# One layer's quantised feed-forward moved into the turns of the attention before it, with GpSimd taking over part of the VectorE work

## The reference, cut to what matters

```python
def xattn0(x, ctx):                      # 16 heads of 64, 256 queries, 64 keys
    scores = q @ k.T * 64 ** -0.5        # causal mask, heads side by side: 16 * 64 = 1024 columns
    return softmax(scores) @ v @ WO
def ffn0(h):                             # h = layer-normed x
    amax  = max(abs(h)) over blocks of 32
    scale = 2 ** (floor(log2(amax)) - 2) * 2 ** (0.5 * tanh(4 * delta))
    q     = fp4_round(clip(h / scale, -6, 6)) * scale
    return q @ quantised_weight.T + bias
x = x + tanh(g) * xattn0(layernorm(x), ctx)
x = x + tanh(g) * ffn0(layernorm(x))
```

## Time and profile before

| | us |
|---|---|
| three timed runs | 1154.90, 1156.94, 1159.53 (median 1156.94) |
| the profiled execution: its time, and its span | 1150.98, 1149.2 |
| busy in the span: TensorE, VectorE, ScalarE, GpSimd | 1009.0, 755.2, 491.6, 360.2 |
| granted TensorE clock, mean | 0.932 |
| share of the chain that ended last: TensorE, VectorE, ScalarE, DMA | 67%, 20%, 4%, 4% |

### The profile page before, as it was taken

One profiled execution on the slowest core, in us unless ns is written; L12 is line 12 of the kernel. 1 busy time (PEld: TensorE's weight loads), 2 busy tenths in 40 slices (PEclk: granted clock), 3 DMA queues, 4 the chain that ended last, 5 costly groups with the idle time before them and its releaser, 6 DMA issues.

```text
span 1149.2 us, 17589 instructions
## 1 busy us (share of the span) xinstructions
PE 1009.0 (88%) x6266; PEld 612.9 (53%) x6273; DVE 755.2 (66%) x2259; ACT 491.6 (43%) x951; POOL 360.2 (31%) x406
## 2 busy tenths in 40 slices
PE   9999999985499998899889999999999995399980
PEld 6355665664344445434776666665544443177750
DVE  2657767779976677685777655555678787444334
ACT  2655555554334442364224333332344442266534
POOL 0060000003332283312343422100425765356670
PEclk7999999995699998899989999999999997799995
DMA  8075000004000003000003444433000101501116
GB/s 195 1 271 154 1 1 1 1 6 87 1 2 1 1 1 118 1 0 1 1 1 77 98 93 95 86 75 75 1 1 25 34 32 41 209 30 36 35 45 225
DMA packets 37846, 61.99 MB, mean 54 GB/s; under 512 B 6049, under 2 KB 22152, under 8 KB 36994
## 3 DMA queue, kind: packets, MB, share of 16 engines
q1 hardware_dynamic: 33154, 52.40, 16.8%
q0 software_dynamic: 4608, 8.50, 2.3%
HBM read 40.47 MB, written 21.45 MB: 54 GB/s over the span
## 4 chain that ended last, share of the span: by engine, by line
PE 67%; DVE 20%; ACT 4%; DMA 4%; issue 3%; POOL 1%; SPq 0%; DVEq 0%; POOLq 0%; ACTq 0%
PE bank L1148 8%; PE bank L1210 6%; PE bank L585 5%; PE bank L490 5%; PE bank L447 5%; PE bank L1164 5%; PE bank L1221 3%; PE bank L651 3%; PE bank L418 3%; PE bank L476 2%; PE bank L483 2%; DVE nmax L2099 2%; ACT att L1386 2%; DMA big_a<-gates 1%; PE bank L604 1%
## 5 line engine op out<-in xcount | busy, mean ns | idle before, releaser
L1148 PE MATMUL bank<-big_b 128*128 128x512 f32 x288 | 135.8, 596 | 0.0
L2099 DVE TENSOR_REDUCE nmax<-bank 128x16 f32<-128x1024 f32 x64 | 77.9, 1218 | 46.6 <-PE bank L591 28.6
L1703 POOL TENSOR_SCALAR xn<-xw,mean,rstd 128x128 f32<-128x128 f32 x62 | 49.5, 808 | 181.5 <-DVEq L2674 90.4
L1600 ACT ACTIVATE att<-bank 128x512 f32<-128x512 f32 (+1 forms) x72 | 43.0, 597 | 134.4 <-PE bank L1148 131.9
L1874 POOL DMA_INDIRECT expert_outs<-big_a,big_b x80 | 77.7, 971 | 56.0 <-DVE big_a L2748 32.9
L1164 PEld LDWEIGHTS bank<-big_b,att 128*128 128x128 f32 (+1 forms) x576 | 72.9, 191 | 31.8 <-issue 19.1
L2610 DVE TENSOR_TENSOR att<-att,bank 128x512 f32<-128x512 f32 (+1 forms) x72 | 49.2, 684 | 57.0 <-PE bank L1164 54.2
L1164 PE MATMUL bank<-big_b,att 128*128 128x128 f32 (+1 forms) x576 | 77.9, 278 | 3.5 <-DVE xw L1978 2.2
L1386 ACT ACTIVATE att<-bank 128x1024 f32<-128x1024 f32 x64 | 62.0, 1021 | 41.4 <-PE bank L627 41.4
L1865 POOL DMA_INDIRECT expert_rows<-xw,big_b x64 | 63.7, 995 | 50.6 <-DVEq L2201 34.1
L1210 PE MATMUL bank<-big_b 128*128 128x384 f32 (+1 forms) x192 | 72.8, 522 | 0.7 <-ACT big_b L1627 0.7
(11 more groups left out here) (423 smaller groups left out, 2166.5 us busy)
## 6 DMA issues: line engine op xcount, KB each, us to landing
big_a<-gates SPq DMA_DIRECT2D x14, 1024.0 KB, 9.8
expert_rows<-big_b SPq DMA_DIRECT2D x1, 5240.0 KB, 19.6
expert_outs<-big_b SPq DMA_DIRECT2D x1, 4096.0 KB, 31.9
big_a<-expert_outs SPq DMA_DIRECT2D x6, 512.0 KB, 8.4
big_a<-expert_rows SPq DMA_DIRECT2D x1, 2620.0 KB, 13.8
big_a<-in_mask SPq DMA_DIRECT2D x2, 1024.0 KB, 12.2
big_b<-in_w_in SPq DMA_DIRECT2D x1, 2048.0 KB, 8.1
out<-xw SPq DMA_DIRECT2D x8, 256.0 KB, 2.4
```

The lines of the kernel that those rows point to most:

```text
L1148: mm = nc.tensor.matmul(bank[2 * (n % 3) + k][:, :], w13[:, k, c * 128:(c + 1) * 128], xnT_all[:, g * GW:(g + 1) * GW], start=True, stop=True)
L1703: ins = nc.gpsimd.tensor_scalar(xn[:, b % 2, j], x[:, t], mean[:, t:t + 1], rstd[:, t:t + 1], SUB, MUL)
L2099: nc.vector.tensor_reduce(nmax[:, j], psum[:, 2048:3072].rearrange("p (h t) -> p h t", t=T), AX.X, MAX, negate=True).then_inc(s.free, 1)
```

## The change

Groups 0 to 5 of layer 0's feed-forward run inside turns 3 to 15 of its attention; groups 6 and 7 remain behind it. Group g is normalised in turn 2g+3 (ScalarE, `ffn_norms`) and its scales found there (VectorE, `block_scales`); it is rounded in turn 2g+4 (`rounded`), and transposed and multiplied in two halves in turns 2g+5 and 2g+6 (`half_transposes`, `half_products`), each half followed by its own residual sum on VectorE (`half_output`). GpSimd gets four tasks in the attention: in each turn it normalises the second tile's probabilities; in each even turn it makes mean and inverse root of one group of tiles (`statistics0`, 23 small instructions in a chain) and then multiplies a rounded group by its scale and adds the bias (`rescaled`); in each odd turn it multiplies by the inverse scale (`unscaled`). The mask is loaded in turn 3 and converted in turns 8, 10, 12 and 14. `unrounded` moves from `big_a` to `big_b`. The core of the diff:

```diff
@@ PE, attention0 @@
+                    if b == 1:
+                        weights_transpose()
+                    if b > 4:
+                        half_transposes(*divmod(b - 5, 2))
                     pe.wait_ge(s.v_evac, 2 * b + 2)
                     pe.wait_ge(s.normed, 2 * b + 1)
                     chunk_transposes(0, 0)
                     chunk_transposes(0, 1)
                     if b + 1 < B:
                         score(b + 1, 1, 1).then_inc(s.scores, 1)
+                    if b > 4:
+                        half_products(*divmod(b - 5, 2))
@@ ACT, attention0 @@
                     if b + 2 < B:
                         norms(b + 2)
+                    if b == 1:
+                        weights_evac()
+                    if b > 2 and b % 2:
+                        ffn_norms((b - 3) // 2)
+                    if b > 7 and b % 2 == 0:
+                        masks((b - 8) // 2)
+                    if b > 4:
+                        half_evac(*divmod(b - 5, 2))
                     turned_evac(b, 0)
                     turned_evac(b, 1)
@@ POOL @@
+            def statistics0(g):
+                ...
+                pool.wait_ge(att_sems.nmax, 2 * g + 4)
+                step(tt(apart, me, mo, SUB))
+                ...
+                for _ in range(3):
+                    step(tt(apart, r, r, MUL))
+                    step(tt(apart, apart, v, MUL))
+                    step(ts(apart, apart, -0.5, 1.5, MUL, ADD))
+                    step(tt(r, r, apart, MUL))
+                step(tt(square, mu, r, MUL))
+                ts(square, square, -1.0, None, MUL).then_inc(att_sems.ready, 1)
+            def attention0(s):
+                for b in range(B):
+                    p = probs[:, 1].rearrange("p (h t) -> p h t", t=T)
+                    pool.wait_ge(s.summed, b + 1)
+                    nc.gpsimd.tensor_tensor(p, p, rsum[:, 1, H:2 * H].unsqueeze(2).broadcast_to([128, H, T]), MUL) \
+                        .then_inc(s.normed, 1)
+                    if b > 1 and b % 2 == 0:
+                        statistics0(b // 2 - 1)
+                    ...
+                    if b > 2 and b % 2:
+                        unscaled((b - 3) // 2)
+                    if b > 3 and b % 2 == 0:
+                        rescaled(b // 2 - 2)
@@ POOL, main @@
             blank_rows()
             spread_keys(g1)
+            attention0(att_sems)
             pool.wait_ge(layer_done, 1)
             similarity_keys()
@@ DVE, attention0 @@
                     step(nc.vector.tensor_reduce(rsum[:, j, 0:H], p, AX.X, ADD))
+                    if j:
+                        nc.vector.reciprocal(rsum[:, j, H:2 * H], rsum[:, j, 0:H]).then_inc(s.summed, 1)
+                        return
@@
-                    else:
-                        ...
-                        moments_of(settled)
-                        first_root(settled)
-                        better_root(settled)
+                    if b > 2 and b % 2:
+                        block_scales((b - 3) // 2)
+                    if b > 3 and b % 2 == 0:
+                        rounded(b // 2 - 2)
                     for j in range(2):
-                        ...
                         dve.wait_ge(s.o, 2 * b + j + 1)
                         residual(0, 2 * b + j, bank[7 - 3 * j][:, 0:128], s.o_read, 2 * b + j + 1, statistics=False)
+                        if b > 4 and j == 0:
+                            half_output(*divmod(b - 5, 2))
```

More of the change, by code:

```diff
@@ L346, in _ @@
                          blank[:, 0, 0:D].unsqueeze(1).broadcast_to([128, TOP3 * NT, D])).then_inc(dma_fill, 16)
+            sp.wait_ge(att_sems.scores, 2 * TPG)
+            for half in range(2):
+                sp.dma_start(mask_int[64 * half:64 * half + 64, :].rearrange("p (b s) -> p b s", b=B),
+                             A["mask"]).then_inc(dma_w[1], 16)
+            sp.wait_ge(dma_w[1], 2 * 16)
             sp.wait_ge(layer_done, 1)
@@ L428, in layer1_key, with weights_transpose, half_transposes, half_products @@
                                  start=True, stop=True).then_inc(keys_mm, 1)
+            def weights_transpose():
+                pe.wait_ge(weights_ready, 2)
+                nc.tensor.transpose(bank[6][:, 0:128], wq0[:, :], ident[:, :]).then_inc(kernel0_mm, 1)
+            def half_transposes(g, half):
+                pe.wait_ge(q_done, 2 * g + 2)
+                for j in range(2):
+                    mm = nc.tensor.transpose(bank[6][:, j * 128:(j + 1) * 128], xn[:, 1, 2 * half + j], ident[:, :])
+                mm.then_inc(q_xT, 1)
+            def half_products(g, half):
+                pe.wait_ge(q_xT_evac, turned_to(g, half))
+                if g or half:
+                    pe.wait_ge(q_o_read, turned_to(g, half) - 1)
+                for j in range(2):
+                    at = (2 * half + j) * 128
+                    mm = nc.tensor.matmul(bank[7][:, (1 + j) * 128:(2 + j) * 128], xnT[:, 1, at:at + 128], wq0T[:, :],
+                                          start=True, stop=True)
+                mm.then_inc(q_o, 1)
             def attention0(s, G):
@@ L830, in transposes @@
                 def transposes(g):
-                    pe.wait_ge(q_done, g + 1)
+                    pe.wait_ge(q_done, 2 * g + 2)
                     for j in range(TPG):
@@ L1434, in quantised_ffn @@
             def quantised_ffn():
[L1435 to L1457 removed]
+                half_evac(HALVED - 1, 1)
                 similarity_row()
@@ L1730, in mumoe @@
+            def quantised_ffn():
+                rescaled(NG - 2)
+                pool.wait_ge(att_sems.ready, readied(NG - 1))
+                for j in range(2):
+                    ins = nc.gpsimd.tensor_scalar(xn[:, 0, j], x[:, j], mean[:, j:j + 1], rstd[:, j:j + 1], SUB, MUL)
+                ins.then_inc(narrow.xn, 1)
+                unscaled(NG - 1)
+                rescaled(NG - 1)
             def mumoe():
@@ L2304, in quantised_ffn @@
             def quantised_ffn():
[L2305 to L2312 removed]
                 def output(g):
                     dve.wait_ge(biased, g + 1)
[L2316 to L2317 removed]
+                    dve.wait_ge(q_o, turned_to(g))
+                    residual(1, TPG * g, bank[1][:, :], q_o_read, turned_to(g), tiles=TPG)
                 ends, last = None, slice(NT - 2 * TPG, NT)
+                step(nc.vector.drain())
+                moments_of(ends)
+                first_root(ends)
+                for _ in range(3):
+                    better_root(ends)
+                stt(lnt[:, 2, last], mean[:, last], -1.0, rstd[:, last], MUL, MUL).then_inc(att_sems.ready, 1)
+                rounded(NG - 2)
+                half_output(HALVED - 1, 1)
+                block_scales(NG - 1)
                 step(nc.vector.memset(vals[:, 0:4, :], 0.0))
@@ L2323, in quantised_ffn @@
                 step(ins)
-                group(0)
-                for g in range(NG - 1):
-                    group(g + 1)
-                    output(g)
-                    if g == 2:
-                        moments_of(ends)
-                        first_root(ends)
-                        for _ in range(3):
-                            better_root(ends)
-                        stt(lnt[:, 2, last], mean[:, last], -1.0, rstd[:, last], MUL, MUL).then_inc(att_sems.ready, 1)
+                rounded(NG - 1)
+                output(NG - 2)
                 return output
```

208 lines of the change are left out of this document (113 added, 95 removed).

## The result

The kernel after takes 1142.66 us, the median of 15 runs (1135.31 to 1152.32); the kernel before, beside it, 1155.26 us (15 runs, 1152.11 to 1163.46). The ratio is 0.9887, with a 95% interval from 0.9856 to 0.9918: faster by 12.6 us or 1.1%, where 1155 us was forecast and 1140 to 1170 given as the range. The profiled execution took 1148.19 us with a span of 1146.4.

The account below looks back on a forecast made before the run. TensorE was taken to bound the attention turns and VectorE the feed-forward. A saving of 39.1 us against added waits, work and clock summed to -1.5 us, 1149.5 from 1150.98; with timed runs 6 us higher, 1155 us was stated, range 1140 to 1170.

Parts of the forecast that it names:

- the rivals at 1141: The two rival outcomes forecast at 1141 us, GpSimd in time and no wait in turn 0; chance together 0.31.
- what goes away behind the attention: After the attention's end: the last rounding comes 18.9 us behind it instead of 58.0, saving 39.1 us.
- turn 0, wait and clock: Turn 0: TensorE waits 13.0 us for GpSimd's normalisation behind the loop of 16, plus 1.7 us for the clock's fall.
- TensorE's added work, turns 5 to 14: Two transposes and two products more a turn, 0.67 us in each of 10 turns, 6.7 us.
- waits in the odd turns: Turns 5, 7, 9, 11 and 13: TensorE's half transposes wait 1.7 us each for `rescaled`, 8.4 us.
- clock in the odd turns: TensorE's clock falls after the wait in half of the five odd turns, at 1.7 us each: 4.2 us.
- last turn: Last turn: TensorE's second-tile transposes come at 10.0 us instead of 6.4, costing 3.6 us.
- Each holds the other up: Even turns: VectorE's five roundings and GpSimd's chain delay each other; roundings take 3.6 us, 6 of 23 chain instructions get done.
- GpSimd in time: Rival: GpSimd's small operations aren't held up or cost under 0.2 us, so odd-turn waits go; 1141 us, chance 0.25.
- GpSimd late: Rival: a small GpSimd operation with its semaphore costs 0.4 us, slower than before; 1171 us, chance 0.22.
- No wait in turn 0: Rival: GpSimd's part in turn 0 is out of the way, 14.7 us less; 1141 us, chance 0.06.

Follow-up runs that it names:

- GpSimd's normalisation alone: Kernel before, with only the second tile's normalisation given to GpSimd in all 16 turns, feed-forward not moved: 1170.48 us, ratio 1.0129 to before.
- turn 0 on VectorE: Kernel after, but VectorE normalises the second tile in turn 0 and GpSimd only from turn 1: 1125.78 us, ratio 0.9749 to before.
- early statistics: Kernel after, with GpSimd's chain of 23 waiting for VectorE's token statistics instead of the split of the maxima: 1133.67 us, ratio 0.9826 to before.
- the fourth round: Kernel after, with a fourth refinement of the inverse root, 27 instead of 23 instructions in GpSimd's chain: 1148.09 us, ratio 0.9938 to before.
- both normalisations on VectorE: Kernel after, but VectorE makes both normalisations in all turns and GpSimd keeps its other three tasks: 1139.79 us, ratio 0.9870 to before.

## Why the prediction was right, and where it was not

The places of the gain and of the waits were right, and the measured time lies in the range. The size was short by some 12 us: 1142.66 us lies outside the 1147 to 1163 that my own sum allowed, and inside the stated range only because that reached down to the rivals at 1141. That the likeliest number was on the faster side at all is partly luck: -1.5 us was less than the 5.8 us that I held to be no change. My chances don't quite follow from their working either: it gives about 0.33 for faster, 0.25 for slower and 0.41 for no change, where I stated 0.38, 0.27 and 0.35. By the terms of the sum, in us, from the profile of after (turn lengths against those of before):

| term | forecast | measured |
|---|---|---|
| what goes away behind the attention | -39.1 | -40.8 (63.06 to 22.26) |
| turn 0, wait and clock | +14.7 | +14.1 (12.81 to 26.91) |
| TensorE's added work, turns 5 to 14 | +6.7 | +6.6 (0.66 a turn) |
| waits in the odd turns | +8.4 | +4.5 (four of 0.81, turn 5 with 1.25) |
| clock in the odd turns | +4.2 | 0 |
| last turn | +3.6 | +2.9 (11.57 to 14.43) |
| turn 1 | 0 | -0.3 (12.58 to 12.30) |
| sum | -1.5 | -13.0 |

**Right, and shown by experiments.** The price of turn 0: its mechanism by GpSimd's normalisation alone (+14.1 us there too) and by turn 0 on VectorE. The wait in odd turns as the end of the chain: by early statistics (gone) and the fourth round (+1.15 a turn). The spacing of 0.28 us against my 0.29 was as taken, and so was the chain's start, 8.96 us into the turn against 8.9. Counting by starts and not by lengths was what mattered: at a length of 0.20 the 18 that run behind the roundings would seem to take 3.6 us instead of 5.0.

**Right in the profile.** The way behind the attention: the last rounding ends 18.6 us behind its end, 18.9 was forecast. Of the further 1.4 us of gain, behind that rounding, 0.9 is the last products' clock (L882, 1.16 us for 8; in before, 2.08).

**The step that failed first** was "Each holds the other up: the roundings take about 2.8 + 5 x 0.16 = 3.6 and end at 12.4". I had a row in which VectorE waits for GpSimd and one in which GpSimd waits for VectorE, and let both happen at once. They took 2.79 us and ended 11.59 us into the turn. That 0.8 us comes straight off the wait of 1.7 and leaves 0.9; measured is 0.8 in four turns. GpSimd got 5 done in that time, one for each rounding, where I gave it 6 in a longer one; and the later hold-up cost 0.85 where I took 1.1. These two offset each other. So odd turns took 13.66 us, where I gave 14.5 or more.

**The second was the clock** in the odd turns. I let it fall in half of them; it fell in none, not even with pauses of 1.74 and 2.17 us (the fourth round). It did fall behind a pause of 2.49 us, in turn 5 with both normalisations on VectorE. A single pause's length is not enough to go by, as the earlier trace rows against the fourth round show.

**The base was sound.** I added the 6 us by which the timed median lay above the profiled execution of before. With the measured sum, 1150.98 - 13.0 = 1138, and 6 more give 1144, where 1142.66 was measured. The miss is in the terms, above all in the two named here.

**The rivals.** GpSimd in time (1141 us) comes nearest in number, but not in its mechanism: small operations were held up by VectorE and did cost 0.28, and the wait was there, at about half its size (4.5 us of 8.4). GpSimd late fell: 0.28 is under the 0.31 from which it decides. No wait in turn 0 fell. Of a code table's load there is nothing to be seen: the chain's first instructions in turn 2 stand at 110.17, 110.45 and 110.75, with the reload between the last two.

**Open.** Why the last turn still waits 0.97 us for `rescaled` with early statistics was not tested. In the trace TensorE, with no scores to make, asks at 266.31, and the chain ends only at 266.21 with `rescaled`, 1.05 us long, behind it. Nor was it shown why the stage in layer 2 is granted a clock of 0.76 in one execution and 0.90 in another, or whether the change has a part in it; none of the runs changed it on purpose.

## What to carry to other kernels

When work is given to an idle engine, look first at what stands ahead of it on that engine's queue at the first turn: one instruction behind a loop of 17 us cost 14 us, as much as all other costs of the interleaving together, and giving that turn back to VectorE took it away and kept the rest. For a chain of small dependent instructions, count starts to starts, find the semaphore that it really needs (its start was 2.3 us sooner here), and ask which engine comes first where the two hold each other up: in the roundings the engine whose instructions stood back to back was not held up, and only the other paid. Take terms from a table by stage, not from the difference of two whole executions, when a later stage takes 51.6 us in one profile and 59.8 in another.

## What the runs showed of the hardware

- GpSimd's instruction on 4 columns takes 0.19 to 0.22 us and 0.28 us to the next dependent one; beside VectorE's roundings it lasts to the end of the running one (0.32 to 0.63 us), beside VectorE's 1.23 us normalisation 1.05 to 1.21. GpSimd's normalisation of 1024 columns takes 1.90 us, where VectorE takes 1.23.
- A stream of VectorE instructions beside such a chain wasn't lengthened (2.79 us for five). VectorE instructions that came while a longer GpSimd one ran were: 1.60 us instead of 0.17 on 16 columns beside a 1.90 us one, 1.69 instead of 1.23 beside a 1.05 us one.
- VectorE's reductions (L2172) and its residual sums from a bank (L2076) did not hold the chain up (0.19 to 0.22 us beside them).
- TensorE's clock stayed at full through pauses of 0.58, 1.02, 1.74 and 2.17 us in otherwise busy turns, and was at half behind ones of 2.49 and 12.56 us. In the last turns it was full right behind pauses of 1.54 us (before), 0.97 (early statistics) and 4.21 (after), and fell after that.
